# A convolution residual and a GRU on one core: the prologue reordered, W_ih and step 0's x products ahead of the load of x

## What is computed

```python
x = x + conv(x, cond[:, None, :]) + conv_b      # depthwise, causal, 128 taps over 64 steps
h = cond                                        # 128 x 512
for t in range(64):
    gi = x[:, t] @ W_ih + b_ih                  # 512 x 1536
    gh = h @ W_hh + b_hh
    r = sigmoid(gi_r + gh_r); z = sigmoid(gi_z + gh_z)
    n = tanh(gi_n + r * gh_n)
    h = (1 - z) * n + z * h
    out[:, t] = x[:, t] + h
```

## Time and profile before

| | us |
|---|---|
| median of three runs | 1267.79 |
| lowest, highest | 1265.87, 1269.69 |
| the profiled execution, its own time | 1266.82 |
| its span in the trace | 1265.0 |
| TensorE matmul, busy | 1180.7 (93%) |
| VectorE, busy | 536.7 (42%) |
| ScalarE, busy | 491.9 (39%) |
| GpSimd, busy | 18.9 (1%) |
| moved by DMA | 98.18 MB, mean 78 GB/s |

### The profile page before, as it was taken

How to read it: one execution, slowest core, us unless ns; L and a number is a source line. 1 busy time by engine, 2 the same in 40 slices (tenths; PEclk the granted TensorE clock), 3 DMA queues, 4 the chain that set the end, 5 groups by cost and what they waited for, 6 DMA issues and landing times.

```text
span 1265.0 us, 14934 instructions
## 1 busy us (share of the span) xinstructions
PE 1180.7 (93%) x5520; PEld 982.5 (78%) x5520; DVE 536.7 (42%) x803; ACT 491.9 (39%) x928; POOL 18.9 (1%) x18
## 2 busy tenths in 40 slices
PE   2239999999999999999999999999999999999997
PEld 1228788888878888888888888888888888888886
DVE  1044666767656433333333333333333333333333
ACT  0041677777767333332333333322323333323332
POOL 1040000000000000000000000000000000000000
PEclk7669999999999999999999999999999999999999
DMA  9987988889894211111100111111100111111000
GB/s 117 166 202 155 181 176 184 184 187 189 187 186 123 68 34 34 33 33 33 33 25 27 31 33 33 33 33 33 31 25 28 33 33 33 33 33 33 25 19 23
DMA packets 307251, 98.18 MB, mean 78 GB/s; under 512 B 237584, under 2 KB 303632, under 8 KB 305168
## 3 DMA queue, kind: packets, MB, share of 16 engines
q1 hardware_dynamic: 295152, 94.67, 35.3%
q10 hardware_dynamic: 12064, 3.05, 1.9%
HBM read 63.34 MB, written 34.34 MB: 77 GB/s over the span
## 4 chain that ended last, share of the span: by engine, by line
PE 86%; DMA 3%; ACTq 3%; DVE 2%; ACT 2%; SPq 2%; issue 1%; POOL 0%; DVEq 0%
PE bank L708 78%; PE bank L730 4%; DMA bias_hn<-in_L_cond_b_hh_dram 2%; PE bank L675 2%; ACTq L442 2%; SPq L305 1%; DVE w_ih_lo L255 1%; PE bank L698 1%; ACT tmp L503 1%; DMA kernel_full<-k_full 1%; ACT x_parts L493 1%; ACT bank L469 1%; SPq L316 0%; DVE early_result L581 0%; DMA xT<-xres 0%
## 5 line engine op out<-in xcount | busy, mean ns | idle before, releaser
L708 PE MATMUL bank<-w_ih_hi,xT_hi 128*128 128x512 f32 x768 | 306.3, 399 | 0.0
L708 PE MATMUL bank<-w_ih_lo,xT_hi 128*128 128x512 f32 x768 | 300.2, 391 | 0.0
L708 PE MATMUL bank<-w_ih_hi,xT_lo 128*128 128x512 f32 x768 | 300.1, 391 | 0.0
L708 PE MATMUL bank<-w_hh_hi,hT_hi 128*128 128x512 f32 x768 | 299.6, 390 | 0.0
L708 PE MATMUL bank<-w_hh_lo,hT_hi 128*128 128x512 f32 x768 | 299.6, 390 | 0.0
L708 PE MATMUL bank<-w_hh_hi,hT_lo 128*128 128x512 f32 x768 | 298.8, 389 | 0.0
L708 PEld LDWEIGHTS bank<-w_ih_hi,xT_lo 128*128 128x128 f32 x768 | 144.4, 188 | 31.3
L708 PEld LDWEIGHTS bank<-w_hh_hi,hT_lo 128*128 128x128 f32 x768 | 144.2, 188 | 30.5
L708 PEld LDWEIGHTS bank<-w_hh_hi,hT_hi 128*128 128x128 f32 x768 | 144.4, 188 | 28.1
L708 PEld LDWEIGHTS bank<-w_hh_lo,hT_hi 128*128 128x128 f32 x768 | 144.4, 188 | 27.6
L708 PEld LDWEIGHTS bank<-w_ih_hi,xT_hi 128*128 128x128 f32 x768 | 144.8, 189 | 26.8 <-ACT bank L469 0.3
(11 more groups left out here) (50 smaller groups left out, 794.8 us busy)
## 6 DMA issues: line engine op xcount, KB each, us to landing
x_unit<-in_x_dram SPq DMA_DIRECT2D x64, 256.0 KB, 4.8
toep_ring<-kernel_parts SPq DMA_DIRECT2D x128, 128.0 KB, 3.4
out_dram<-outZ SPq DMA_DIRECT2D x256, 64.0 KB, 1.6
xT<-xres SPq DMA_DIRECT2D x63, 256.0 KB, 2.7
xres<-stage SPq DMA_DIRECT2D x32, 384.0 KB, 4.8
x_early<-in_x_dram SPq DMA_DIRECT2D x8, 512.0 KB, 15.5
xres<-early_result SPq DMA_DIRECT2D x32, 128.0 KB, 2.8
w_ih_raw<-in_L_cond_W_ih_dram SPq DMA_DIRECT2D x16, 192.0 KB, 13.5
```

The costliest lines, as they stand in the source:

```text
L708: mm = nc.tensor.matmul(psum[:, :], a[:, rows], b[w][:, cols], start=False, stop=stop and n == 2, skip_group_check=True)
```

## The change

- SP's queue: rows of `cond` whole, the last 16 tap rows, the x row whole, W_ih by gate (12 DMAs: for each gate 4 with 2 KB runs), the four bias loads (moved here from ScalarE's queue), x for 16 steps, the Toeplitz blocks, W_hh by gate (R, N, Z). The last two stand behind waits for the zeroed buffer and the stored taps.
- The Toeplitz blocks come from `tap_pad`, a 32 x 512 DRAM tensor that holds the last 16 tap rows (1 is added to the last of them) and 16 rows of zeros. A group's DMA gathers by tap: for each partition and each output, a run of 64 channels, 256 B. In `toep_early` the channel is therefore innermost, and the stationary of channel g is read with a step of 64 values.
- The rows of `cond` and x, now loaded whole, are put in channel order by a VectorE copy and a ScalarE copy. `kernel_full` in DRAM and its 4 stores are gone, and so are the 16 Toeplitz loads of ScalarE's queue.
- PE: the x products of step 0, gate by gate, stand before the early convolution. The matmuls that open the banks use hT_hi.
- ScalarE: W_ih's high parts before the bias copies; W_hh's after them. VectorE: all low parts of W_ih first, then one eviction ahead of each part of W_hh, the last four evictions at the end. GpSimd takes the low parts of block k = 3 instead of those of gate N, 3 of each matrix instead of 4.
- After the early convolution GpSimd clears the ring that the bulk blocks use, and SP waits for that before it loads units.

```diff
         @block.sync
-            load_row(h, taps, h0_loaded)
-            load_row(x_row, x[:, 0, :], x_row_loaded)
+            sp.dma_start(h0[:, :], taps).then_inc(h0_loaded, 16)
+            sp.dma_start(tap_rows[:, :], taps[K - EARLY:K, :]).then_inc(tap_rows_loaded, 16)
+            sp.dma_start(x_row[:, :], x[:, 0, :]).then_inc(x_row_loaded, 16)
+            def load_weights(w, matrix):
+                for g in GATES[w]:
+                    for q4 in range(QUADS):
+                        sp.dma_start(
+                            raw[w][q4 * QUAD:(q4 + 1) * QUAD, :].rearrange("r (k n) -> r k n", k=KB)[:, :, g:g + D],
+                            matrix[q4 * P:(q4 + 1) * P, g:g + D].rearrange("(k r) n -> r k n", r=QUAD),
+                        ).then_inc(raw_loaded[w][g // D], 16)
+            load_weights(0, w_ih)
+            for tile, source in ((bias_rz, b_ih[0:N]), (bias_tmp, b_hh[0:N]),
+                                 (bias_in, b_ih[N:NG]), (bias_hn, b_hh[N:NG])):
+                sp.dma_start(tile[:, :], source.partition_broadcast(P)).then_inc(bias_loaded, 16)
             for c in range(C0):
                 sp.dma_start(
                     x_early[c * EARLY:(c + 1) * EARLY, :].rearrange("s (b g) -> s b g", g=G0),
...
-            for w, matrix in ((0, w_ih), (1, w_hh)):
-                for k in range(KB):
-                    for q4 in range(QUADS):
-                        row = q4 * P + k * QUAD
-                        sp.dma_start(raw[w][q4 * QUAD:(q4 + 1) * QUAD, k * NG:(k + 1) * NG],
-                                     matrix[row:row + QUAD, :]).then_inc(raw_loaded[w][k], 16)
+            sp.wait_ge(toep_zeroed, 2)
+            sp.wait_ge(tap_pad_stored, 16 * 2)
+            for c in range(C0):
+                first = tap_pad[:, c * G0:(c + 1) * G0]
+                sp.dma_start(
+                    toep_early[c * EARLY:(c + 1) * EARLY, c * EARLY * G0:(c + 1) * EARLY * G0].rearrange(
+                        "s (u g) -> s u g", g=G0),
+                    bass.AP(first.tensor, first.offset, [[D, EARLY], [D, EARLY], [1, G0]]),
+                ).then_inc(toep_early_loaded, 16)
+            load_weights(1, w_hh)
...
             sp.wait_ge(early_done, NB0)
+            sp.wait_ge(toep_cleared, 1)
         @block.gpsimd
...
+            pool.wait_ge(early_done, NB0)
+            nc.gpsimd.memset(toep_early[:, 0:T_RING * TOEP], 0.0).then_inc(toep_cleared, 1)
         @block.scalar
+            act.wait_ge(tap_rows_ready, 1)
+            act.dma_start(tap_pad[0:EARLY, :], tap_rows[:, :]).then_inc(tap_pad_stored, 16)
...
+            high_weights(0)
             act.wait_ge(bias_rz_ready, 1)
             act.wait_ge(banks_opened, 1)
             put_bias(ps_r, bias_rz[:, R:R + D], bias_r_put)
...
+            act.wait_ge(k_parts_stored, 16 * QUADS)
+            high_weights(1)
         @block.vector
-            evicted = 0
             for n, (w, k, g) in enumerate(W_PARTS):
-                if g == R:
-                    for _ in range(2):
-                        early_evict(evicted)
-                        evicted += 1
+                if 0 <= n - KB * 3 < KB * 3:
+                    early_evict(n - KB * 3)
                 if not on_pool(w, k, g):
                     dve.wait_ge(w_hi_ready, n + 1)
                     low_weights(nc.vector, w, k, g).then_inc(w_lo_ready, 1)
-            assert evicted == NB0
+            for n in range(KB * 3, NB0):
+                early_evict(n)
         @block.tensor
+            for psum, gate, put in ((ps_r, R, bias_r_put), (ps_z, Z, bias_z_put), (ps_in, N, bias_in_put)):
+                pe.wait_ge(put, 1)
+                for k in range(KB):
                     low_weights_ready(0, k, gate)
+                    mm = block_product(psum, xT_hi, xT_lo, 0, gate, k, gate == N and k == KB - 1)
             mm.then_inc(gi_done, 1)
+            pe.wait_ge(toep_early_loaded, 16 * C0)
+            pe.wait_ge(x_early_loaded, 16 * C0)
+            pe.wait_ge(y0_ready, KB)
+            for g in range(G0):
+                n, slot = g * B // BANK, g * B % BANK
+                if slot == 0 and n >= 3:
+                    pe.wait_ge(early_evicted, n - 2)
+                mm = nc.tensor.matmul(conv_bank[n % 3][:, slot:slot + B],
+                                      toep_early.rearrange("p (m g) -> p g m", g=G0)[:, g, :],
+                                      x_early[:, :].rearrange("p (b g) -> p g b", g=G0)[:, g, :],
+                                      start=True, stop=True)
```

More of the change, by code:

```diff
@@ L99, in conv_residual_gru @@
     toep_at = top[0]
-    toep_ring = place("toep_ring", T_RING * 2 * BLOCK * P, F32R)
-    toep = [toep_ring[:, n * 2 * BLOCK * P:(n + 1) * 2 * BLOCK * P] for n in range(T_RING)]
+    toep_span = place("toep_span", G0 * P, F32R)
     toep_end = top[0]
+    TOEP = 2 * BLOCK * P
+    toep = [toep_span[:, n * TOEP:(n + 1) * TOEP] for n in range(T_RING)]
+    top[0] = toep_at + T_RING * TOEP * KW
     parts = [place(f"x_parts{n}", BLOCK * 2 * B, F32R) for n in range(HL_RING)]
@@ L136, in conv_residual_gru @@
     k_parts = place("k_parts", KB * 2 * P, F32R)
-    x_row = place("x_row", D)
+    x_row, h0 = place("x_row", D), place("h0", D)
+    x_row_by_k = place("x_row_by_k", D)
+    tap_rows = place("tap_rows", D, parts=EARLY)
+    tap_zeros = place("tap_zeros", D, parts=EARLY)
+    lag0_row = place("lag0_row", 8, parts=EARLY)
     bias_tmp = place("bias_tmp", N)
@@ L157, in conv_residual_gru @@
         x_early_loaded = sem("x_early_loaded")
-        toep_early_loaded = [sem(f"toep_early_loaded{n}") for n in range(2)]
+        toep_early_loaded = sem("toep_early_loaded")
         bias_loaded = sem("bias_loaded")
@@ L239, in split_block @@
             return m // 2 + 2
-        W_PARTS = [(w, k, g) for w in range(2) for k in range(KB) for g in (R, Z, N)]
+        GATES = ((R, Z, N), (R, N, Z))
+        W_PARTS = [(w, k, g) for w in range(2) for g in GATES[w] for k in range(KB)]
         def w_cols(k, g):
@@ L427, in _ @@
             act.wait_ge(hT_done, 1)
[L428 removed]
+            act.wait_ge(k_zeroed, 1)
             nc.scalar.activation(tap_columns(k_full)[:, :, 0:T], tap_columns(ps_hT)[:, :, T:P],
                                  ACT.Copy).then_inc(k_full_copied, 1)
+            nc.scalar.activation(hT_hi[:, :], ps_hT[:, :], ACT.Copy).then_inc(hT_hi_ready, 1)
             act.wait_ge(k_full_ready, 1)
[L432 to L434 removed]
@@ L465, in _, with high_weights @@
             nc.scalar.activation(xT_hi[:, :], xT[0][:, :], ACT.Copy).then_inc(xT_hi_ready, 1)
-            nc.scalar.activation(hT_hi[:, :], ps_hT[:, :], ACT.Copy).then_inc(hT_hi_ready, 1)
+            act.wait_ge(k_lo_ready, 1)
+            for q4 in range(QUADS):
+                act.dma_start(kernel_parts.rearrange("(q k r) l j -> q r k (l j)", k=KB, r=QUAD)[q4],
+                              k_parts[q4 * QUAD:(q4 + 1) * QUAD, :].bitcast(F32).rearrange("r (k e) -> r k e", k=KB)
+                              ).then_inc(k_parts_stored, 16)
             def put_bias(psum, bias, done):
                 nc.scalar.activation(psum[:, :], bias, ACT.Copy).then_inc(done, 1)
+            def high_weights(which):
+                for w, k, g in W_PARTS:
+                    if w != which:
+                        continue
+                    if k == 0:
+                        act.wait_ge(raw_loaded[w][g // D], 16 * QUADS)
+                    cols = w_cols(k, g)
+                    nc.scalar.activation(hi[w][:, cols], raw[w][:, cols], ACT.Copy).then_inc(w_hi_ready, 1)
+            high_weights(0)
             act.wait_ge(bias_rz_ready, 1)
```

110 lines of the change are left out of this document (43 added, 67 removed).

## The result

The change makes the kernel faster: 1260.57 us against 1267.43 us for the kernel before on the same chip (medians of five runs each), a ratio of 0.9944 with a 95% interval of 0.9930 to 0.9959, or 6.9 us. The profiled execution took 1261.43 us (span 1259.6), the slowest of its five; the profiled execution of before took 1266.82 (span 1265.0).

What follows compares the result with a forecast made beforehand. TensorE bounds the 64 recurrent steps, so only the dense part's start, about 105.8 us, can move. Gains of 7.6 (convolution end) and 0.5 (after it) make 8.1: 1266.8 - 8.1 = 1258.7, plus the median's 1.0, 1259.7 us; range 1253 to 1271.

Steps and rivals of the forecast that it cites:

- the likeliest case: Whole kernel: faster than before by more than 0.3%, within 1253 to 1265 us; chance 70%.
- Convolution start, 70: Early convolution: starts at about 70 instead of 52.5 us, after rows, W_ih, biases, x and Toeplitz blocks in SP's queue.
- 235 GB/s: Loads ahead of x: rate with both queues at work, giving 9.2 us for biases, split kernel and padded taps.
- The cover of the x products: Step 0's x products, moved ahead of the convolution: end near 45 to 50 us, 20 us before it starts.
- Rival B, x at 90 GB/s: Load of x: slow even without Toeplitz packets, convolution starts near 81 and ends at 109, kernel 1270.7 us; chance 7%.
- Rival C, W_hh late: Evictions: W_hh's three gates land together near 84, evictions stop at number 1, about 1267.5 us, no change; chance 10%.
- Convolution length, 28.2: Early convolution: 128 records at 0.22 us run unbroken, ending at 98.2 against 105.85 us, a gain of 7.6.
- I take no cost, as both reads overlap now: Convolution's strided weight load: at most 0.22 us, hidden behind the moving read's 0.22, so it adds nothing.
- Rival A: Convolution's 128 records: strided weight loads don't hide, up to 0.22 us each, 1288 us; decides from pitch 0.28; chance 13%.
- The rule of lines cited with the forecast: Convolution's weight loads: SBUF lines are 16 bytes, each crossing pays; up to 28 us worse if read ports don't overlap.
- After the convolution, 0.5: Steps 0 to 2 after the convolution: moving the 8.2 us of x products gains 0.5 us, bounds 0 and 2.7.
- The wait of 5.5: Step 0 after the convolution: TensorE comes 8.2 us sooner and waits about 5.5 for ScalarE's bias copy.

## Why the prediction was right or wrong

The forecast was 1259.7 and the time 1260.57, inside the range, and faster, as the likeliest case said. The direction rests on a mechanism that the runs bear out, the new order closing the hole. That the number came out so near is luck: two terms were each off by over 7 us, with opposite signs.

- *Convolution start, 70.* It was 62.8. Rows, W_ih, biases and what goes beside them were put at 6 + 13.7 + 9.2 = 28.9; in after the last bias landed at 25.5, when GpSimd's add begins. The step that failed is that 235 GB/s, read from a stretch of weight loads, holds for the biases and the stores beside them: the stretch in which they move shows 374. Of its 1.87 MB the stores on ScalarE's queue are 0.49; whether it is they or the broadcast of the biases to 128 partitions that makes the difference isn't shown. x and the blocks, put at 40.5 and rounded up by 0.6, took 37.3 from there, in part because x already began to flow beside the biases. The cover of the x products was wider than said: they end at 40.1, 23 us ahead of the convolution.
- *Rival B, x at 90 GB/s.* Wrong, 120. The run with the old gather bears out the forecast's reason for leaving it: x moves at 89 beside 64 B packets and at 119 without them.
- *Rival C, W_hh late.* Wrong. Gate R's first high part began at 67.5, the eviction behind it was at 68.8, and there was no hole.
- *Convolution length, 28.2.* From the first record to the next matmul it was 35.7, and the step that failed is "I take no cost, as both reads overlap now". That a stride doubles a read was right for either operand alone at 2.4 GHz (0.11 with both side by side, 0.22 with one stride, whichever). That a slower weight load hides behind the slower moving read was wrong by 0.06 a record: 0.28 is less than the 0.44 of two reads one after the other and more than the 0.22 of two that don't disturb each other. Rival A had the place, the bounds (0 and 0.22) and the point from which it decides, 0.28, which is just what was measured. It didn't turn the sign only because the start came 7.2 earlier. The rule of lines cited with the forecast, by which a strided weight load pays, points the right way: it paid 0.06 beside a strided moving read and 0.11 beside one side by side at 2.4 GHz. The Trainium skill, SBUF — State Buffer, section "A bandwidth-pool intuition that's wrong (but worth ruling out)", gives TensorE's weight loads a second, independent read port. The runs disagree in this case: with both reads strided they show 0.28, where independent ports would leave 0.22.
- *After the convolution, 0.5.* It was 0.3 to the end of step 0, less than the 1.6 by which this stretch differs between executions. The wait of 5.5 was right (5.58). That the rest would go to the first bulk block and step 2's input was wrong, since SP gets to these 6.7 us earlier too; what took it in the profiled execution was the lower clock after the wait, 2.0 us, at which the prediction put nothing. The run with the products moved back shows that their move is worth nothing measurable.
- *The cause of the gain.* Before, it was 53.2 us from the convolution's first record to the next matmul, for 28.2 of work, so its holes cost 25.0. Of these the later start took back 10.3 and the pitch 7.5, which leaves the 7.2 at its end. The new order closed the holes; the gather by tap did not pay.

How the two reads interfere, that is, at which strides and widths the 0.06 appears, stays open: one stride, 256 B, was tried. So does the share of the bias loads in the gain, as no run moves them alone.

## What to carry to other kernels

A layout that makes a gather cheaper moves a stride into the reader: count how often it is read, and whether the other operand of the same instruction has a stride too. Where the reader is on the path, let an idle engine pay for the stride once, in a copy under a load; that was worth 5.5 to 8 us here on top of the change. Work moved from one gap to another gains only what the first gap doesn't need: look at what it covered at the old place, and at the clock after the wait that it leaves behind.

## What the runs showed of the hardware

- fp32 matmuls, 128 x 128 by 128 columns: with both operands side by side 0.21 us at a granted clock of 0.50 and 0.11 at 1.00; with a 256 B stride in either operand 0.22, with it in both 0.28, at either clock.
- x's packets of 256 B, on 16 partitions a DMA, move at 119 to 120 GB/s, whether one queue issues them or two; its packets of 128 B at 77; beside 64 B packets on the other queue those of 256 B move at 89.
- After TensorE's wait of 5.58 us its granted clock was 0.50, which cost 2.0 us in that execution (after waits of 5.7 us in two others, 13 and 6 products ran at the low clock); with the products in that place it stayed at 1.00.
